# Score products on two 64-row tiles of TensorE, issued term by term in turns

## The reference

```python
xn = _layernorm(x)
x = x + attn(xn, Wq, Wk, Wv, Wo) + ffn(xn, fast_b, w_fc, w_proj, u, v, gate)
# attn: retention with 8 heads of 16 features, in chunks of C tokens
attn = einsum('bhid,bhjd->bhij', qc, kc) * D        # scores, decayed and causal
o_intra = einsum('bhij,bhje->bhie', attn, vc)
o_inter = einsum('bhid,bhde->bhie', qc * decay_q, S)
S_new = decay_s * S + einsum('bhjd,bhje->bhde', kc * decay_k, vc)
# ffn: r = relu(h); out = bitlinear(r * r, w_proj), with ternary weights
```

## Time and profile before

| | |
|---|---|
| median of 3 runs | 179.24 us (179.17 to 181.82) |
| span of the profiled execution, first to last instruction | 177.4 us |
| TensorE busy | 157.6 us, 89% of the span |
| VectorE busy | 137.3 us, 77% |
| ScalarE busy | 78.8 us, 44% |
| GpSimd busy | 61.0 us, 34% |

### The profile page before, as it was taken

The page is one execution under the profiler, slowest core; times in us unless marked ns, Lnnn a source line. Parts: engine busy times, 40 slices in busy tenths (PEclk is TensorE's granted clock), DMA queues, the critical chain, the costliest instruction groups (busy, mean ns, idle before and its releaser), DMA issues.

```text
span 177.4 us, 3389 instructions
## 1 busy us (share of the span) xinstructions
PE 157.6 (89%) x1177; PEld 122.1 (69%) x1177; DVE 137.3 (77%) x343; ACT 78.8 (44%) x155; POOL 61.0 (34%) x46
## 2 busy tenths in 40 slices
PE   1561298799999999999999999999999999999992
PEld 0240295577887788787878787878787877788771
DVE  6889898789867988788768876887789757764551
ACT  2510276471277316732583238423762177217710
POOL 8699700065005600380019000920074005500550
PEclk9999999999999999999999999999999999999998
DMA  4970041205240333024301521061005210431001
GB/s 156 431 299 0 0 64 56 59 4 81 37 124 0 60 60 118 0 43 75 114 5 26 92 73 45 7 104 60 6 0 89 33 59 0 74 48 61 0 4 59
DMA packets 7913, 11.65 MB, mean 66 GB/s; under 512 B 1296, under 2 KB 5520, under 8 KB 7776
## 3 DMA queue, kind: packets, MB, share of 16 engines
q1 hardware_dynamic: 7584, 10.82, 25.4%
q10 hardware_dynamic: 320, 0.72, 1.2%
HBM read 5.50 MB, written 2.10 MB: 43 GB/s over the span
## 4 chain that ended last, share of the span: by engine, by line
PE 81%; DVE 13%; DMA 2%; issue 1%; ACT 1%; DVEq 0%
PE ps_o L696 10%; PE ps_score L634 10%; PE ps_score L636 8%; PE ps_score L635 8%; PE ps_work L635 6%; PE ps_work L634 6%; PE ps_work L636 6%; PE ps_y L706 4%; PE ps_y L708 4%; DVE q_dec L453 4%; PE ps_o L685 4%; PE ps_state L688 3%; PE ps_work L656 3%; PE ps_work L630 2%; DMA x_in<-x_tok 2%; PE ps_work L657 2%
## 5 line engine op out<-in xcount | busy, mean ns | idle before, releaser
L301 POOL TENSOR_TENSOR sq_lo<-square,sq_hi 128x512 fp32r<-128x512 f32 x32 | 42.4, 1347 | 107.5 <-ACT sq_hi L369 106.7
L481 DVE TENSOR_TENSOR scores<-ps_score,cst 128x512 f32<-128x512 f32 x64 | 43.8, 686 | 12.6 <-PE ps_score L636 12.5
L365 ACT ACTIVATE square<-ps_work 128x512 f32<-128x512 f32 x32 | 19.0, 599 | 36.3 <-PE ps_work L636 35.6
L634 PE MATMUL ps_score<-q_exp,k_hi 128*128 128x512 f32 x64 | 28.3, 441 | 1.7 <-DVE scores L481 1.7
L636 PE MATMUL ps_score<-q_exp,k_lo 128*128 128x512 f32 x64 | 25.2, 394 | 0.0
L635 PE MATMUL ps_score<-q_exp,k_hi 128*128 128x512 f32 x64 | 25.1, 392 | 0.0
L696 PE MATMUL ps_o<-scores,v_pad 128*32 128x128 f32 x512 | 20.6, 279 | 0.0
L373 ACT ACTIVATE square<-square 128x512 f32<-128x512 f32 x32 | 19.2, 628 | 0.0
L369 ACT ACTIVATE sq_hi<-square 128x512 fp32r<-128x512 f32 x32 | 18.2, 621 | 0.0
L696 PEld LDWEIGHTS ps_o<-scores,v_pad 128*32 128x32 f32 x512 | 12.0, 109 | 7.7 <-issue 5.8
L634 PEld LDWEIGHTS ps_score<-q_exp,k_hi 128*128 128x128 f32 x64 | 12.1, 188 | 6.3 <-issue 3.0
(11 more groups left out here) (94 smaller groups left out, 315.8 us busy)
## 6 DMA issues: line engine op xcount, KB each, us to landing
q_exp<-q_parts SPq DMA_DIRECT2D x60, 64.0 KB, 2.3
x_in<-x_tok SPq DMA_DIRECT2D x8, 256.0 KB, 3.0
resid<-x_feat SPq DMA_DIRECT2D x1, 2048.0 KB, 10.8
out_feat<-resid SPq DMA_DIRECT2D x8, 256.0 KB, 2.1
ffn_in<-ffn_weights SPq DMA_DIRECT2D x1, 576.0 KB, 4.8
cst<-const ACTq DMA_DIRECT2D x1, 468.0 KB, 6.2
wqkv<-qkv_weights ACTq DMA_DIRECT2D x1, 192.0 KB, 5.1
rank_in<-rank_weights ACTq DMA_DIRECT2D x1, 41.1 KB, 2.8
```

The source lines that it names most:

```text
L301: nc.gpsimd.tensor_tensor(sq_lo[:, f, :], square[:, f, :], sq_hi[:, f, :].bitcast(F32), ALU.subtract).then_inc(lo_ready, 1)
L365: nc.scalar.activation(square[:, f, :], ps_work[f % 2][:], ACT.Relu).then_inc(relu_ready, 1)
L481: nc.vector.tensor_tensor(scores[c % 2][:, half * HALF:(half + 1) * HALF], ps_score[half][:].rearrange("p (h i) -> p h i", h=HALF), causal ...
L634: mm(out, w_hi, x_hi, start=True, stop=False)
```

## The change

Each half's score product now uses only the 64 rows on which its queries are not zero: rows 0 to 63 for half 0, rows 64 to 127 for half 1. That places the two halves on two tiles of the array of 64 rows by 128 columns. `score` makes both halves in one call, six matmuls, in turns: term 0 of half 0, term 0 of half 1, term 1 of half 0, and so on. It waits once, for both masks of the chunk before. TensorE's list is written anew around it: a chunk's score is one block, and `own_values`, `project_vk(nxt,0)` and `project_k` are moved. Nothing changes on the other engines.

```diff
-            def score(b, c, half):
-
-                if c == 0 and half == 0:
+            def score(b, c):
+
+                if c == 0:
                     pe.wait_ge(k_lo_ready, b.count(1, 1))
                     pe.wait_ge(q_spread, b.count(16 * H, 16 * H))
-                if c > 0:
-                    pe.wait_ge(scores_ready, b.count(2 * NT, 2 * c + half - 1))
+                else:
+                    pe.wait_ge(scores_ready, b.count(2 * NT, 2 * c))
                 toks = slice(c * CH, (c + 1) * CH)
-                q_hi, q_lo = (q_exp[b.parity][:, half * HALF:(half + 1) * HALF, part, toks] for part in range(2))
-                three_terms(ps_score[half][:], k_hi[:, toks], k_lo[:, toks], q_hi, q_lo).then_inc(scores_done, 1)
+                for term in range(3):
+                    for half in range(2):
+                        rows = slice(half * HALF * DK, (half + 1) * HALF * DK)
+                        keys = (k_hi, k_hi, k_lo)[term][rows, toks]
+                        part = (0, 1, 0)[term]
+                        ins = mm(ps_score[half][:], keys,
+                                 q_exp[b.parity][rows, half * HALF:(half + 1) * HALF, part, toks],
+                                 start=(term == 0), stop=(term == 2))
+                        if term == 2:
+                            ins.then_inc(scores_done, 1)
...
                 hidden(b, 0)
                 hidden(b, 1)
-                score(b, 0, 0)
-                score(b, 0, 1)
+                score(b, 0)
                 hidden(b, 2)
-                score(b, 1, 0)
                 hidden(b, 3)
                 if later > 0:
                     turn_xn(nxt, b)
 
                 pe.wait_ge(w2_copied, 1)
                 carry(b, 0)
-                score(b, 1, 1)
+                score(b, 1)
                 own_values(b, 0)
-                score(b, 2, 0)
                 if later > 0:
                     project_q(nxt, b)
                 carry(b, 1)
+                score(b, 2)
                 own_values(b, 1)
-                score(b, 2, 1)
+                if later > 0:
+                    project_vk(nxt, 0)
                 carry(b, 2)
-                score(b, 3, 0)
-                if later > 0:
-                    project_vk(nxt, 0)
-                score(b, 3, 1)
+                score(b, 3)
+                own_values(b, 2)
                 if later > 0:
                     project_k(nxt)
-                own_values(b, 2)
                 carry(b, 3)
                 own_values(b, 3)
```

More of the change, by code:

```diff
@@ L762, in body @@
                 carry(b, 1)
+                score(b, 2)
                 own_values(b, 1)
-                score(b, 2, 1)
-                carry(b, 2)
-                score(b, 3, 0)
                 if later > 0:
                     project_vk(nxt, 0)
-                score(b, 3, 1)
+                carry(b, 2)
+                score(b, 3)
+                own_values(b, 2)
                 if later > 0:
                     project_k(nxt)
-                own_values(b, 2)
                 carry(b, 3)
```

## The result

The changed kernel takes **191.11 us** (median of 4 runs, 189.97 to 192.47), beside 179.2 for the kernel before on the same chip: ratio 1.069, 95% interval 1.060 to 1.079. It is slower, and 1.2 us from the forecast of 192.3. In the profiled execution the span went from 177.4 to 188.5 us.

What follows compares the result with a forecast made beforehand. TensorE's instruction stream was taken as the bound; -2.33 + 0.5 + 3.8 gives +2.0 us a steady batch, +13.1 in all. On the 177.4 span that is 190.5, plus 1.8 for unprofiled runs: 192.3 us, range 187 to 197.

Steps and rivals of the forecast that it cites:

- The sum: Whole loop: savings, shape changes and waits together add 2.0 us a steady batch, +13.1 over the eight batches.
- the six waits: TensorE in a steady batch: new waits for late results, mostly from VectorE, +3.8 us together.
- Part 1: Score matmuls as pairs on 64-row tiles: a chunk takes 0.81 us instead of 1.39, -2.33 us a batch.
- stagger of 0.116: Score pairs: the second tile runs half a slot, 0.116 us, behind the first because of its own weight load.
- Rival 3: Score tiles: next weight load can't start while the tile's matmul runs; pair 0.34, +3.0 a batch, 200 us; chance 0.14.
- rival 4: Score pairs don't overlap at all: no gain, +4.1 us a batch, 208 us; chance 0.07.
- Part 2: TensorE's changes of tile shape: 13 a batch instead of 8, five more at 0.10 us, +0.5 us.
- upper end: Changes of tile shape: +1.3 us a batch if each of the 13 cost 0.2.
- Part 3: TensorE's new order against VectorE's unchanged list: results come late, waits of +3.8 us a steady batch.
- kind end: Steady batch: perfect overlap, no added shape cost; waits grow by the stagger to 4.2, batch 19.95, 188 us.
- First and last batch: The two batches that aren't steady: the first comes to +1.7 us, the last to -0.5 us.
- Rival 1: TensorE's new order: the waits don't come, -1.83 us a batch, 164.6 us; chance 0.12.

Runs made afterwards that it cites:

- e1: Changed kernel with TensorE's new order kept, but scores on full 128-row matmuls, half after half, instead of pairs; 196.75 us, ratio 1.099 to the kernel before.
- e4: Changed kernel with VectorE's list moved to match TensorE's new order; 175.36 us, ratio 0.979 to the kernel before.
- e3: Changed kernel with one move on VectorE, decay_q(nxt) ahead of mask(2,0); 190.53 us, ratio 1.062 to the kernel before.
- e6: On top of e4, TensorE's list spread, second product cut into eight matmuls, VectorE's inverse-root steps moved late; 169.36 us, ratio 0.943 to the kernel before.
- e2: Changed kernel with the score loops swapped, all terms of half 0 then of half 1, still 64-row tiles; 191.64 us, ratio 1.066 to the kernel before.
- e8: Kernel before the change with only chunk 0's two score products made as pairs on 64-row tiles, nothing moved; 178.45 us, ratio 0.997.
- e7: On top of e3, GpSimd's subtraction cut from 512 to 8 columns, sq_hi used for sq_lo, timing only; 183.3 us, ratio 1.022 to the kernel before.

## Why the prediction was right, and where its sizes were off

**The sum.** Predicted +13.1 for the loop and +2.0 for a steady batch; measured +13.2 and +1.86 (18.54 to 20.40). The preparation, which the prediction held fixed, was 2.1 us shorter in the profiled execution and covers the 1.2 us by which the time lies below the forecast. The mechanism was the one forecast: e1 shows it without the pairs, and e4 removes most of it by VectorE's list alone. Five of the six waits came where they were expected.

**Part 1, the pairs.** Predicted 0.81 a chunk, with the second tile 0.116 behind; measured 0.80, made otherwise. The six starts of the block at 93.48 lie at 0, 0.003, 0.333, 0.338, 0.564 and 0.568 us: the tiles run together, 12 slots in place of 24. The stagger of 0.116 that the sum had isn't there, and the first pair is 0.10 longer, because the weights of the second were not loaded ahead (their loads start 0.11 behind the first pair), which the sum did not have. Two errors of 0.1 cancelled. Rival 3 (0.34 a pair) and rival 4 are out: a pair after the first takes 0.23, and the load of its successor starts with it:

```profile
93.81 0.19 PEld L674 LDWEIGHTS ps_score<-q_exp,k_lo 64*128 64x128 f32 x2
```

The rule of the Trainium skill that the prediction names under rival 3, by which this load would have had to wait for the tile's matmul, is not borne out for tiles either: the second pair of matmuls starts at 93.81 too, and this load runs beside it.

**Part 2, changes of shape.** The step in is 0.09 (89.79 to 90.11, less 0.23), as predicted. The way out into a full-array matmul costs 0.20, not 0.10: 0.09 before it and 0.11 behind it (91.01 to 91.35). In and out of `own_values` it stays at 0.10 each. Only the block of chunk 0 goes straight into a full-array matmul, so this is 0.1 a batch; the prediction's upper end had it.

**Part 3, the waits, in a steady batch.**

| wait | predicted | measured |
|---|---|---|
| `project_q` for `low_xn` | 0.98 | 1.26 |
| `project_vk(0)` for `decay_q` | 0.78 | 0.87 |
| `score(3)` for `mask(2,1)` | 1.03 | 0.75 |
| `own_values(3)` for the masks | 0.2 | 0 |
| `project_vk(1)` for `low_k` | 0.5 | 0.70 |
| `turn_xn` for the relu | 0.2 | 0.17 |
| sum | 3.7 (3.8 with the reload) | 3.75 |

`project_q` waits 0.28 longer than predicted. Of this, 0.12 is the missing stagger: TensorE leaves the pairs, and so `own_values`, that much earlier (the prediction's kind end said so). The other 0.16 is that it starts 0.24 after the end of `xn_lo` (95.96 to 96.20), not 0.08, where `project_vk(0)` starts 0.05 after `q_dec`. It has three semaphore waits in a row ahead of it, but these alone are not the reason: with the same three, the `project_q` of the seventh batch starts 0.10 after its `xn_lo` (157.24 to 157.34). The cause stays open.

The predicted wait of `score(3)` was too long by the 0.28 that `low_q` no longer stands: in the new order it doesn't meet GpSimd (0.69 in the timeline above, 0.97 in the earlier trace rows). For the same reason the `inverse_root` between the masks of chunk 3 takes 0.15 instead of 0.53, and `own_values(3)` doesn't wait; `project_vk(1)` behind it waits those 0.2 longer instead. The prediction took both durations as fixed, from rows in which another engine held them up. The sum came right because the errors went both ways. The measured terms give 18.54 - 2.36 + 0.6 + 3.75 = 20.5, 0.1 more than the batch; a full 512-column slot is a little shorter in it (0.229 us over the eleven from 106.52 on, against 0.234 before), and 29 of them make about that 0.1. Why it is shorter isn't shown.

**First and last batch.** Predicted +1.7 and -0.5; measured +2.5 and -0.4. The three waits of the last batch came at 0.41, 0.40 and 0.39 (0.4, 0.4 and 0.5 in the prediction). The first batch began at a lower clock:

```profile
24.70:30.50 5.80, 5.78 (x15) 3.80 (x16) 5.13 (x29) 2.46 (x6) 0.00 (x0) 0.50 0.14 41
```

The granted clock is 0.50 of 2.4 GHz in this stretch, the lower level of 1.2 GHz, and the trace shows what came before: TensorE had waited 3.9 us for `k_tok`. A 512-column slot took 0.42 us there (25.32 to 25.74) instead of 0.23:

```profile
25.32 0.63 PE L635 MATMUL ps_work<-xn_lo,w_hi 128*128 128x512 f32 x1
25.74 0.63 PE L636 MATMUL ps_work<-xn_hi,w_lo 128*128 128x512 f32 x1
```

From the start of `hidden` 0 to that of `hidden` 3 the batch took 5.86 us, where e4, at full clock, took 3.58. In return the wait of `score` for a late mask, which the prediction kept (1.7 us before, 1.2 in e3), isn't there. The prediction had no term for the clock, and it isn't bound to the change: e4 has the same order of TensorE and the same pairs and no such stretch.

**The rivals.** Rival 1 (164.6 us, the waits don't come) gave a mechanism that is real only once VectorE's list is moved and work is spread over the gaps: e6 comes to 169.4 by it. In the table of four batches above, the new lists gain only together. That the ledger was accurate to 0.15 us a batch is partly luck, as said; the sign was not, since the waits (3.75) are twice what the pairs save with their changes of shape (about 1.8).

## What to carry to other kernels

When two engines each walk a list written out by hand, a block moved in one list changes what the other must deliver next: go through the partner's list for each moved block and see what stands ahead of the one result that is wanted, and move that too. Work that is saved on the full engine was also somebody's cover; price a saving only after redoing the arrival times, and look for work that can be split and laid into the gaps, as the second product was. And a duration read from a trace may hold another engine's: compare the instruction's shortest case with its usual one before it goes into a sum.

## What the runs showed of the hardware

- Two matmuls on 64-row tiles into two banks start a few ns apart (3 in the median of the kernel after, at most 10) and take one slot of 0.23 us together. When the program has one half behind the other (e2), the block is as short.
- A block on 64-row tiles pays 0.09 us to enter, about 0.10 for its own first exposed weight load, 0.09 to leave and 0.11 for the exposed load of the full-array matmul behind it (e8).
- A VectorE instruction with two SBUF inputs took 0.68 us with GpSimd out of the way and 1.64 beside GpSimd's subtraction, and GpSimd's next subtraction, which met it, 1.72 instead of 1.28 (e3, e7).
- In the preparation, a VectorE `TENSOR_SCALAR` stands until GpSimd's memset of `q_exp[1]`, 14.2 to 21.1 us, is over, and with it those queued behind it, whose records overlap it. Which one it is differs. The kernel before, after (four instructions in one row), and e1, VectorE's first such row each:

```profile
13.12 8.05 DVE L543 TENSOR_SCALAR wo_scaled<-ffn_in,inv_scale 128x128 f32<-128x128 f32 x1
```

```profile
16.80 5.82 DVE L555 TENSOR_SCALAR q_exp<-q_parts,cst 128x512 fp32r<-128x512 f32 x4
```

```profile
12.91 8.23 DVE L529 TENSOR_SCALAR fc_above<-ffn_in,half_scale,scale 128x128 f32<-128x128 f32 x1
```

The loop then starts at 26.87, 24.73 and 28.95 us. The earlier in VectorE's list the instruction stands that meets the memset, the more is queued behind it. The code of these instructions is the same in all three kernels, and why another one meets the memset isn't shown: in the kernel after, `wo_scaled` begins at 13.10 too and is done after 1.19 us. So 4 us between two profiles can come from here; that is why the loops were compared, and not the spans alone.
